# Attention on one core: the maxima turned later, the loads cut in four, two buffers of sums

## The chip, the cores and the metric

The kernel runs on one core of a Trainium2 chip. The metric is the device time of one execution, in microseconds. The core has TensorE (PE), VectorE (DVE), ScalarE (ACT), GpSimd (POOL), and SyncE (SP), which here issues nearly all transfers.

## The reference

One decoder layer on x of 2 x 2048 x 512 in fp32: causal self-attention, cross-attention over 77 rows, and a mixture of eight experts, each followed by a layer norm of x plus the result. Only the first is touched:

```python
qkv = x @ Wqkv.T
q, k, v = map(merge_heads, jnp.split(qkv, 3, axis=-1))     # 16 heads of 32
dots = jnp.einsum('bhid,bhjd->bhij', q, k) * dh ** (-0.5)
dots = jnp.where(causal_mask, -jnp.inf, dots)
out = jnp.einsum('bhij,bhjd->bhid', jax.nn.softmax(dots, axis=-1), v)
```

## The kernel before

Three stages follow one another: the projections to q, k and v, which go to DRAM in fp16 parts (`project`), the self-attention (`self_attention`), and everything after it (`chains`). The change is in the second.

The attention works on eight *groups*, each four heads of one batch. The group's q and k lie in one of two pairs of buffers (`q_pair`, `k_pair`), v in `v_sb`. Each of q and k is there in an upper and a lower fp16 part, so a product runs over 96 partitions. A group has four *chunks* of 512 queries; chunk c needs 4(c+1) tiles of 128 keys (`KU`), 40 tiles in all, and 160 *items*, one for each tile and head (`VU`).

Two streams run side by side on PE. The *value stream*, one item a step: PE computes scores with keys on partitions into `st_ps` (line 846), ACT takes the exponential into `probs` (line 743), PE multiplies by v into `o_ps` (line 866). The sums over keys: POOL adds two of three tiles of `probs` into `total` (line 630), PE takes the third tile, and `total` at the end of the chunk, with a column of ones into `den_ps` (lines 880 and 890). Five tiles of `probs` and three banks each of `st_ps` and `s_ps` are there.

The *aux stream* finds the row maxima some 70 items ahead: PE computes scores with queries on partitions into `s_ps` (line 829), DVE reduces them to `seg_max` (line 779). After the last maximum of a chunk comes the item `rows`: DVE takes the maximum over segments (line 783), scales it and splits it into two fp16 parts (lines 785 and 788), PE turns them by four fp16 products (line 818), DVE copies them to `max_rows` (line 775), and SP moves them into two more partitions of `q_pair` (line 671), so that the score product subtracts the maximum. `schedule()` spreads the aux items over the value steps by estimated costs; `done_by(s)` says how many are done by step s.

At the end of a chunk: ACT copies `o_ps` to `o_raw` and `den_ps` to `den`; SP moves `den` into a small layout (line 692), DVE takes reciprocals (line 797), SP stores them and loads them back broadcast as `inv` (lines 696 and 702), POOL multiplies (`o_sb`, line 640), ACT takes the upper fp16 part (line 758), POOL the lower one (line 645), SP stores both (line 709). The steps at which this happens, counted from the chunk's last item, are the constants `TAKEN` to `STORED`.

Order: every engine goes through the same steps in program order (`laps`), a lap of two groups, four times, and waits on semaphores. `chunk_at(s, lag)` tells whether step s lies `lag` steps after the last item of a chunk. Six steps after a group's end SP loads the group after the next into the buffers come free, 24 loads of 128 KB and one of 1 MB (lines 683 to 688).

Of the kernel before, what the change touches and what calls it, by code (L numbers as in the profile page):

```python
# [13 lines left out]
P = 128  # L14
KT = D // P
HG = P // DH
# [385 lines left out]
def self_attention(nc, S, x_rows, q_parts, k_parts, v_rows, o_parts, inv_rows):  # L402
# [16 lines left out]
    AUX = []  # L419
    for c in range(CPB):  # L420
        AUX += [("max", c, (j, h, s)) for j in range(TT) for h in range(HG) for s in range(c + 1)] + [("rows", c, None)]
# [17 lines left out]
    STORED = SCALED + 4  # L439
    TAIL = STORED + 1  # L440
    READY = 6
# [4 lines left out]
    def schedule():  # L446


        off = lambda c, kt: max(kt - c * TT, 0) * P
        steps = [0.06 + 0.6 * (CH - off(c, kt)) / CH for c, kt, _ in VU]  # L450
        busy = [0.0] * NVU
        for t in LAST_TILE:
            busy[(t * HG + HG - 1 + INVERTED) % NVU] += 0.2
        cost = []
        for what, c, unit in AUX:
            if what == "rows":
                cost.append(2.4)
# [78 lines left out]
    with ExitStack() as stack:  # L536
        sb = lambda *a: stack.enter_context(nc.sbuf_tensor(*a))
        ps = lambda *a: stack.enter_context(nc.psum_tensor(*a))
        q_pair = [sb(f"q_pair{a}", [NM, HG, T], F16) for a in range(2)]
# [3 lines left out]
        total = sb("total", [P, HG, CH], F32)  # L543
# [3 lines left out]
        ident16 = sb("ident16", [P, P], F16)  # L547
        future_f = sb("future_f", [P, 2, P], F32)
        future = sb("future", [P, 2, P], BF16)
        seg_max = sb("seg_max", [P, HG, TT, CPB], F32)  # L550
        row_max = sb("row_max", [P, HG, TT], F32)
        max_parts = sb("max_parts", [P, 2, HG, TT], F16)
        max_rows = sb("max_rows", [2 * HG, 2, CH], F16)
# [28 lines left out]
        steps = Count(nc, stack, "steps", 2 * 2 * CPB)  # L582
# [7 lines left out]
        def _(pool):  # L590
# [13 lines left out]
            nc.gpsimd.tensor_copy(ident16[:], ident_f[:]).then_inc(const_ready, 1)  # L604
            nc.gpsimd.tensor_copy(future[:], future_f[:]).then_inc(const_ready, 1)

            pool.wait_ge(const_ready, 3)
# [8 lines left out]
            def step(i, s, first, end):  # L616
                k = tile_at(s, 1, first, end)
                if k is not None and k % NKU in ADDS:
                    c, n = KU[k % NKU][0], adds_upto(k) - 1
                    starts = k % NKU == POOLED[c][1]  # L620
                    pool.wait_ge(exp_done.sem, exp_done.at(i, HG * k + HG - 1))
                    off = max(KU[k % NKU][1] - c * TT, 0) * P
                    if starts:

                        pool.wait_ge(den_ready.sem, den_ready.at(i, k // NKU * CPB + c - 1))
                        other = probs[:, (k // NKU * NKU + POOLED[c][0]) % NP]
                    else:
                        pool.wait_ge(added.sem, added.at(i, n - 1))
                        other = total[:]
                    last = nc.gpsimd.tensor_tensor(total[:, :, off:], other[:, :, off:], probs[:, k % NP, :, off:],  # L630
                                                   ALU.add)
                    if starts and off:
                        last = nc.gpsimd.tensor_copy(total[:, :, 0:off], other[:, :, 0:off])
                    last.then_inc(added.sem, 1)
                c = chunk_at(s, SCALED, first, end)
                if c is not None:

                    pool.wait_ge(inv_loaded, 16 * HG * (2 * CPB * i + c + 1))
# [3 lines left out]
                c = chunk_at(s, SCALED + 3, first, end)  # L642
# [8 lines left out]
        def _(sp):  # L651
            def load(g, a, c):
# [3 lines left out]
                for pair, parts, order in ((k_pair[a], k_parts, (0, 0, 1)), (q_pair[a], q_parts, (0, 1, 0))):  # L656
                    for r, part in enumerate(order):
                        sp.dma_start(pair[r * DH:(r + 1) * DH, :, c * CH:(c + 1) * CH],
                                     parts[part, bass.ds(f, P), cols].rearrange("(h p) n -> p h n", p=DH)).then_inc(
                                         qk_loaded[a][c], 16)  # L660
                if c == CPB - 1:
# [3 lines left out]
            def turn(i, n):  # L665
# [3 lines left out]
                at = c % CPB * CH  # L669
                for part in range(2):  # L670
                    sp.dma_start(q_pair[c // CPB % 2][NR + part:NR + part + 1, :, at:at + CH],
                                 max_rows[part * HG:(part + 1) * HG, c % 2]).then_inc(rows_moved[c % 2], 16)

            def step(i, s, first, end):
# [8 lines left out]
                k = tile_at(s, SUMS, first, end)  # L683

                if k is not None and k % NKU == NKU - 1 and end is None:
                    sp.wait_ge(pv_done.sem, pv_done.at(i, k))
                    for c in range(CPB):
                        load(2 * i + k // NKU + 2, k // NKU % 2, c)
# [10 lines left out]
                if c is not None:  # L699
                    sp.wait_ge(inv_stored, 16 * (2 * CPB * i + c + 1))  # L700
                    for h in range(HG):
                        sp.dma_start(inv[h * DH:(h + 1) * DH, c % 2], inv_rows[c % 2, h].partition_broadcast(
                            DH)).then_inc(inv_loaded, 16)
# [14 lines left out]
            for c in range(CPB):  # L718
                load(1, 1, c)
# [6 lines left out]
        def _(act):  # L726
# [3 lines left out]
            o_hi_done.lead(act)  # L730

            def step(i, s, first, end):
                p = unit_at(s, 0, first, end)
# [20 lines left out]
                c = chunk_at(s, SCALED + 2, first, end)  # L754
# [4 lines left out]

            laps(act, step)  # L760

        @block.vector
        def _(dve):
            for count in (s_read, max_ready, steps, recips):
                count.lead(dve)

            def aux(i, n):
# [4 lines left out]
                if what == "rows":  # L772

                    dve.wait_ge(rows_moved[k % 2], stored_at(2 * (CPB * i + k // 2)))
                    nc.vector.tensor_copy(max_rows[:, k % 2], s_ps[0:2 * HG, slot]).then_inc(s_read.sem, 1)
# [3 lines left out]
                nc.vector.reduce_max(seg_max[:, h, j, s:s + 1], s_ps[:, slot, 0:width], AX.X).then_inc(s_read.sem, 1)  # L779
                if AUX[(n + 1) % NAUX][0] == "rows":  # L780

                    dve.wait_ge(s_read.sem, s_read.at(i, n))
                    nc.vector.reduce_max(row_max[:], seg_max[:, :, :, 0:c + 1], AX.X).then_inc(steps.sem, 1)
                    dve.wait_ge(steps.sem, steps.at(i, 2 * k))
                    nc.vector.tensor_scalar(max_parts[:, 0], row_max[:], -1.0 / QK, None,
                                            ALU.mult).then_inc(steps.sem, 1)
                    dve.wait_ge(steps.sem, steps.at(i, 2 * k + 1))
                    nc.vector.scalar_tensor_tensor(max_parts[:, 1], row_max[:], -1.0 / QK, max_parts[:, 0], ALU.mult,
                                                   ALU.subtract).then_inc(max_ready.sem, 1)
# [14 lines left out]
        def _(pe):  # L804
# [3 lines left out]
            def aux(i, n):  # L808
# [18 lines left out]
                q0 = c * CH + j * P  # L827
                diagonal = s == c
                last = nc.tensor.matmul(s_ps[:, slot, 0:width], q_pair[a][0:NR, h, q0:q0 + P],  # L829
# [6 lines left out]
            def scores(i, p):  # L836
                c, kt, h = VU[p % NVU]
                a, slot = p // NVU % 2, p % (2 * NVU) % RING
                if kt == h == 0:
# [7 lines left out]
                                        q_pair[a][:, h, c * CH + off:(c + 1) * CH], start=True, stop=not diagonal)  # L847
# [35 lines left out]
            def totals(i, c):  # L883
# [5 lines left out]
                for h, out in enumerate(heads):  # L889
                    last = nc.tensor.matmul(den_ps[out, :], ones[:], total[:, h], start=opens, stop=True)  # L890
# [21 lines left out]
            pe.wait_ge(const_ready, 3)  # L912
# [672 lines left out]
```

## Time and profile before

| | us |
|---|---|
| median of three runs (2863.28 to 2868.97) | 2864.77 |
| the profiled execution | 2857.15 |
| its span | 2855.3 |
| PE busy in the span | 2498.4 |
| DVE, POOL, ACT busy | 1760.9, 1120.8, 1103.1 |

The page gives one profiled execution: the busy time of each engine, the span in slices, the chain that ended last, and the costliest groups of instructions. A timeline row is start, duration, engine, line, operation, operands, a count, and in brackets the engine's idle time before it with what ended it. A matmul's end is modelled.

### The profile page before, as it was taken

The numbers are of one execution on the slowest core, as the hardware profiler recorded it, in microseconds if no ns is written. First come the engines' busy times: TensorE is split into PE (matmuls) and PEld (weight loads), VectorE is DVE, ScalarE is ACT, GpSimd is POOL, SyncE is SP. The second block draws the span as 40 slices with busy tenths as digits, with TensorE's granted clock in tenths as the row PEclk, the third lists the DMA queues.
The fourth block names the chain that finished last, engine by engine and source line by source line (L and its number), as shares of the span: only waits on it lengthen the run. The fifth ranks groups of instructions, "written<-read, shape, count | busy, mean of one in ns | idle before, by whom it ended". The sixth has DMA issues, their size and how long they took to land. (4 is left out here: it accounts for less than half of the span.)

```text
span 2855.3 us, 43249 instructions
## 1 busy us (share of the span) xinstructions
PE 2498.4 (87%) x14164; PEld 1062.2 (37%) x14164; DVE 1760.9 (62%) x2997; ACT 1103.1 (39%) x2034; POOL 1120.8 (39%) x404
## 2 busy tenths in 40 slices
PE   8998787896969787887987569999999999999998
PEld 3443232232323232322331235444454445454543
DVE  5442865674747565665760538676767676777765
ACT  4231254553546454554555123233332323232420
POOL 0000386785858585876878212110201111111100
PEclk9999799897989898998998779999999999999999
DMA  7954403012030302022000310101010100101000
GB/s 239 312 182 140 108 17 68 24 25 64 14 75 17 73 17 67 20 48 73 9 24 8 137 41 1 42 16 42 16 42 16 42 16 7 51 1 56 1 15 15
DMA packets 130874, 155.58 MB, mean 54 GB/s; under 512 B 19966, under 2 KB 98558, under 8 KB 129629
## 3 DMA queue, kind: packets, MB, share of 16 engines
q1 hardware_dynamic: 130653, 152.69, 17.7%
q8 instruction: 132, 2.16, 0.3%
q14 instruction: 89, 0.73, 0.1%
HBM read 99.96 MB, written 52.17 MB: 53 GB/s over the span
## 5 line engine op out<-in xcount | busy, mean ns | idle before, releaser
L779 DVE TENSOR_REDUCE seg_max<-s_ps 128x1 f32<-128x512 f32 (+3 forms) x1280 | 707.1, 604 | 293.6 <-PE s_ps L829 202.9
L743 ACT ACTIVATE probs<-st_ps 128x512 f32<-128x512 f32 (+3 forms) x1280 | 611.0, 536 | 565.3 <-PE st_ps L846 353.6
L630 POOL TENSOR_TENSOR total<-total,probs 128x2048 f32<-128x2048 f32 (+3 forms) x200 | 705.7, 3528 | 98.1 <-ACT probs L743 86.2
L829 PE MATMUL s_ps<-k_pair,q_pair 96*128 96x512 f16 (+3 forms) x1280 | 450.9, 371 | 109.9 <-DVE seg_max L779 96.0
L846 PE MATMUL st_ps<-q_pair,k_pair 98*128 98x512 f16 (+3 forms) x1280 | 453.9, 370 | 70.3 <-ACT probs L743 61.7
L1410 PE MATMUL fps<-x2T,w_p_hi 128*128 128x512 f16 x1024 | 317.3, 379 | 0.0
L866 PE MATMUL o_ps<-probs,v_sb 128*32 128x512 f32 (+3 forms) x2560 | 316.3, 568 | 0.1
L1410 PE MATMUL fps<-w_p_hi,hT 128*128 128x512 f16 x1024 | 306.1, 381 | 0.0
L846 PEld LDWEIGHTS st_ps<-q_pair,k_pair 98*128 98x128 f16 x1280 | 125.1, 100 | 375.7 <-ACT probs L743 256.5
L1114 POOL TENSOR_TENSOR rstd<-rstd,keep_power 128x4 f32<-128x4 f32 x24 | 26.2, 1091 | 556.8 <-DVE rstd L1235 556.8
L829 PEld LDWEIGHTS s_ps<-k_pair,q_pair 96*128 96x128 f16 x1280 | 128.9, 102 | 300.5 <-DVE seg_max L779 223.1
L630 POOL TENSOR_TENSOR total<-probs 128x2048 f32<-128x2048 f32 (+1 forms) x32 | 136.2, 4255 | 230.0 <-PE den_ps L890 209.1
L1129 POOL TENSOR_TENSOR soft<-soft,ssum 128x1232 f32<-128x1232 f32 x32 | 72.9, 2289 | 385.9 <-DVE ssum L1265 385.9
L1372 DVE SCALAR_TENSOR_TENSOR x<-fps,gates_un,x 128x512 f32<-128x512 f32 x256 | 184.0, 746 | 36.0 <-PE fps L1410 33.0
L1197 ACT ACTIVATE hidden<-fps,keep_b_sb 128x512 f32<-128x512 f32 x128 | 86.5, 687 | 303.6 <-PE fps L1410 303.3
L1410 PE MATMUL fps<-w_p_lo,hT 128*128 128x512 f16 x512 | 194.6, 380 | 0.0
L1410 PE MATMUL fps<-x2T,w_p_lo 128*128 128x512 f16 x512 | 194.0, 379 | 0.0
L1361 DVE TENSOR_SCALAR hT<-hidden 128x512 f16<-128x512 f32 x128 | 86.1, 673 | 107.6 <-ACT hidden L1197 107.0
L1410 PEld LDWEIGHTS fps<-x2T,w_p_hi 128*128 128x128 f16 x1024 | 100.2, 98 | 128.8 <-issue 5.9
L1410 PEld LDWEIGHTS fps<-w_p_hi,hT 128*128 128x128 f16 x1024 | 98.1, 98 | 130.9 <-issue 20.7
L1168 ACT ACTIVATE soft<-soft 128x1232 f32<-128x1232 f32 x32 | 39.4, 1230 | 200.5 <-DVE soft L1258 200.5
L832 PE MATMUL s_ps<-future,ident_bf 128*128 128x128 bf16 x512 | 116.3, 228 | 0.0
(163 smaller groups left out, 3434.4 us busy)
## 6 DMA issues: line engine op xcount, KB each, us to landing
k_pair<-k_parts SPq DMA_DIRECT2D x96, 128.0 KB, 4.6
q_pair<-q_parts SPq DMA_DIRECT2D x96, 128.0 KB, 5.6
x_raw<-xT_in SPq DMA_DIRECT2D x8, 1024.0 KB, 6.2
q_parts<-qk_out SPq DMA_DIRECT2D x32, 256.0 KB, 3.6
k_parts<-qk_out SPq DMA_DIRECT2D x32, 256.0 KB, 4.0
piece_raw<-w_in SPq DMA_DIRECT2D x8, 1024.0 KB, 8.9
v_rows<-v_out SPq DMA_DIRECT2D x32, 256.0 KB, 2.1
w_parts<-piece_cut SPq DMA_DIRECT2D x8, 1024.0 KB, 5.8
```

The source lines that it names most:

```text
L630: last = nc.gpsimd.tensor_tensor(total[:, :, off:], other[:, :, off:], probs[:, k % NP, :, off:], ALU.add)
L743: nc.scalar.activation(probs[:, k % NP, h, off:], st_ps[:, p % (2 * NVU) % RING, off:], ACT.Exp, scale=SCALE).then_inc(exp_done.sem, 1)
L779: nc.vector.reduce_max(seg_max[:, h, j, s:s + 1], s_ps[:, slot, 0:width], AX.X).then_inc(s_read.sem, 1)
L829: last = nc.tensor.matmul(s_ps[:, slot, 0:width], q_pair[a][0:NR, h, q0:q0 + P], k_pair[a][0:NR, h, s * CH:s * CH + width], start=True, st ...
L832: last = nc.tensor.matmul(s_ps[:, slot, width - P:width], ident[:], future[:, 0], start=False, stop=True)
L846: last = nc.tensor.matmul(st_ps[:, slot, off:], k_pair[a][:, h, kt * P:(kt + 1) * P], q_pair[a][:, h, c * CH + off:(c + 1) * CH], start=Tr ...
L866: last = nc.tensor.matmul(o_ps[out, off:], v_sb[a][:, kt, out], probs[:, k % NP, h, off:], start=(kt == 0), stop=final)
L1129: nc.gpsimd.tensor_tensor(soft[:, j], soft[:, j], ssum[:, j, :].rearrange("p (h a) -> p h a", a=1).broadcast_to([P, H, S2]), ALU.mult).the ...
L1197: nc.scalar.activation(hidden[:, n % 2], fps[:, (u * NUNIT + f) % FB], ACT.Gelu, bias=W["b1_sb"][:, n:n + 1], scale=UN).then_inc(gelu_done ...
L1361: nc.vector.tensor_scalar(hT[:, 0, e % 2, j], hidden[:, n % 2], XS, None, ALU.mult).then_inc(h_hi.sem, 1)
L1372: nc.vector.scalar_tensor_tensor(x2[q][:, j], bank, gates_un[q][:, j, e:e + 1], x2[q][:, j], ALU.mult, ALU.add).then_inc(added.sem, 1)
L1410: last = nc.tensor.matmul(bank, lhs(a, t), rhs(b, t), start=(n == 0), stop=(n == len(steps) - 1))
```

## The change

- Loads of a group come in four parts, at `REFILLED`: 35, 55, 75 and 95 steps after the last item of the group whose buffers they fill; `v_sb` goes with the first part instead of the last. `q_pair` is laid out by chunk.
- `total` has two buffers, by the parity of the chunk; POOL waits for the sum of two chunks ago.
- The item `rows` of a chunk stands behind the first four maxima of the next chunk (`LATER`), but for the last chunk. `seg_max` has two buffers.
- The turn: PE transposes the fp32 maxima in one product (16 x 128). ACT writes the upper fp16 part to `max_rows` (`upper`), DVE the lower one in one operation. The old lines 785, 788 and 775 are gone. `max_rows` has 16 partitions of 128 columns, so the two row transfers have pieces of 256 B.
- `inv` is loaded by one transfer instead of four. The upper part of the output is taken 6 steps after `SCALED` instead of 2, the lower 8 instead of 3, and it is stored at 9 instead of 4. The planner's cost of a `rows` item is 1.0 (last chunk 2.0) instead of 2.4.

```diff
+    LATER = 4
     for c in range(CPB):
-        AUX += [("max", c, (j, h, s)) for j in range(TT) for h in range(HG) for s in range(c + 1)] + [("rows", c, None)]
+        items = [("max", c, (j, h, s)) for j in range(TT) for h in range(HG) for s in range(c + 1)]
+        AUX += items[:LATER] + [("rows", c - 1, None)] * (c > 0) + items[LATER:]
+    AUX.append(("rows", CPB - 1, None))
+    LAST_MAX = [max(n for n, x in enumerate(AUX) if x[:2] == ("max", c)) for c in range(CPB)]
...
-    STORED = SCALED + 4
+    UPPER = SCALED + 6
+    LOWER = UPPER + 2
+    STORED = LOWER + 1
     TAIL = STORED + 1
+    REFILLED = [TAIL + 20 * c for c in range(CPB)]
...
-                cost.append(2.4)
+                cost.append(1.0 if c < CPB - 1 else 2.0)
...
-                        pool.wait_ge(den_ready.sem, den_ready.at(i, k // NKU * CPB + c - 1))
+                        pool.wait_ge(den_ready.sem, den_ready.at(i, k // NKU * CPB + c - 2))
...
-                if c == CPB - 1:
+                if c == 0:
                     sp.dma_start(v_sb[a][:], v_rows[bass.ds(b * T, T), bass.ds(f, P)].rearrange(
...
-                    sp.dma_start(q_pair[c // CPB % 2][NR + part:NR + part + 1, :, at:at + CH],
-                                 max_rows[part * HG:(part + 1) * HG, c % 2]).then_inc(rows_moved[c % 2], 16)
+                    sp.dma_start(q_pair[c // CPB % 2][NR + part:NR + part + 1, c % CPB].rearrange("a h n -> a (h n)"),
+                                 max_rows[:, c % 2, part]).then_inc(rows_moved[c % 2], 16)
...
-                k = tile_at(s, SUMS, first, end)
-
-                if k is not None and k % NKU == NKU - 1 and end is None:
-                    sp.wait_ge(pv_done.sem, pv_done.at(i, k))
-                    for c in range(CPB):
+                for c in range(CPB):
+                    k = tile_at(s, REFILLED[c], first, end)
+                    if k is not None and k % NKU == NKU - 1 and (end is None or k < 0):
+                        sp.wait_ge(pv_done.sem, pv_done.at(i, k))
                         load(2 * i + k // NKU + 2, k // NKU % 2, c)
...
-                    for h in range(HG):
-                        sp.dma_start(inv[h * DH:(h + 1) * DH, c % 2], inv_rows[c % 2, h].partition_broadcast(
-                            DH)).then_inc(inv_loaded, 16)
+                    sp.dma_start(inv[:, c % 2], inv_rows[c % 2].rearrange("h (a n) -> h a n", a=1).broadcast_to(
+                        [HG, DH, CH])).then_inc(inv_loaded, 16)
...
+            def upper(i, n):
+
+                k = n // NAUX * CPB + AUX[n % NAUX][1]
+                slot = n % (2 * NAUX) % RING
+                act.wait_ge(s_ready.sem, s_ready.at(i, n))
+                act.wait_ge(rows_moved[k % 2], stored_at(2 * (CPB * i + k // 2)))
+                nc.scalar.activation(max_rows[:, k % 2, 0], s_ps[0:HG * TT, slot, 0:P], ACT.Copy,
+                                     scale=-1.0 / QK).then_inc(upper_ready.sem, 1)
+
             def step(i, s, first, end):
+                for n in aux_at(s, first, end):
+                    if AUX[n % NAUX][0] == "rows":
+                        upper(i, n)
                 p = unit_at(s, 0, first, end)
...
-                    dve.wait_ge(rows_moved[k % 2], stored_at(2 * (CPB * i + k // 2)))
-                    nc.vector.tensor_copy(max_rows[:, k % 2], s_ps[0:2 * HG, slot]).then_inc(s_read.sem, 1)
+                    dve.wait_ge(upper_ready.sem, upper_ready.at(i, k))
+                    nc.vector.scalar_tensor_tensor(max_rows[:, k % 2, 1], s_ps[0:HG * TT, slot, 0:P], -1.0 / QK,
+                                                   max_rows[:, k % 2, 0], ALU.mult,
+                                                   ALU.subtract).then_inc(s_read.sem, 1)
...
-                    for j in range(TT):
-                        last = nc.tensor.matmul(s_ps[0:2 * HG, slot, j * P:(j + 1) * P], max_parts[:, :, :, j],
-                                                ident16[:], start=(j == 0), stop=(j == TT - 1), skip_group_check=True)
-                    last.then_inc(s_ready.sem, 1)
+                    nc.tensor.transpose(s_ps[0:HG * TT, slot, 0:P], row_max[:].rearrange("p h j -> p (h j)"),
+                                        ident_f[:]).then_inc(s_ready.sem, 1)
```

## Rows read from the trace of the kernel before

**Rows 1.** The attention stage: length, busy of PE, PEld, DVE, ACT, POOL, clock, DMA

```profile
287.00:1583.00 1296.00, 1053.76 (x6976) 359.92 (x6976) 788.88 (x1440) 652.89 (x1376) 930.41 (x306) 0.90 0.17 41
```

**Rows 2.** Waits, 300 to 1570: total, times, longest

```profile
POOL total L630 <- PE den_ps L890: 209.1, 31, 20.5
...
DVE inv_small L797 <- DMA inv_small<-den: 112.1, 7, 17.2
...
ACT o_out L758 <- POOL o_sb L640: 75.3, 31, 4.8
...
PE s_ps L818 <- DVE max_parts L788: 29.9, 17, 3.0
...
PE den_ps L890 <- POOL total L630: 26.3, 9, 8.9
```

**Rows 3.** Timeline, SP and DVE, end of group 1

```profile
634.28 1.32 SPq L658 DMA_DIRECT2D k_pair<-k_parts  x3
...
648.44 6.24 SPq L692 DMA_DIRECT2D inv_small<-den  x1
...
658.63 0.25 DVE L797 RECIPROCAL inv_small<-inv_small 128x16 f32<-128x16 f32 x1 [17.19 <-DMA inv_small<-den]
```

**Rows 4.** First exponential to item 50: group 7, sum of groups 1 to 7

```profile
1426.10:1472.60 46.50, 38.59 (x264) 14.41 (x263) 26.79 (x50) 24.89 (x57) 35.95 (x16) 0.85 0.09 25
sum 425.40, PE 279.19 PEld 101.49 DVE 188.22 ACT 173.64 POOL 248.17; mean PE 39.88 PEld 14.50 DVE 26.89 ACT 24.81 POOL 35.45
```

**Rows 5.** DMA issues of the page; five microseconds of the load (last: GB/s)

```profile
650.00:655.00 5.00, 0.00 (x0) 0.00 (x0) 0.00 (x0) 0.00 (x0) 0.00 (x0) 0.50 1.05 219
...
v_sb<-v_rows SPq DMA_DIRECT2D x8, 1024.0 KB, 10.3
```

**Rows 6.** Timeline of ACT, POOL and SP, group 7, chunk 1; one window

```profile
1448.07 0.63 ACT L758 ACTIVATE o_out<-o_sb 128x512 f16<-128x512 f32 x1 [3.82 <-POOL o_sb L640]
...
1449.95 0.40 SPq L709 DMA_DIRECT2D o_parts<-o_out  x1
...
1451.41 4.51 POOL L630 TENSOR_TENSOR total<-total,probs 128x2048 f32<-128x2048 f32 x1 [1.48 <-ACT probs L743]
...
1457.91 8.10 POOL L630 TENSOR_TENSOR total<-total,probs 128x2048 f32<-128x2048 f32 x2 [2.00 <-ACT probs L743]
...
1465.97 1.26 POOL L640 TENSOR_TENSOR o_sb<-o_raw,inv 128x512 f32<-128x512 f32 x1
...
1467.27 0.63 ACT L758 ACTIVATE o_out<-o_sb 128x512 f16<-128x512 f32 x1 [4.61 <-POOL o_sb L640]
...
1468.66 0.49 ACT L743 ACTIVATE probs<-st_ps 128x128 f32<-128x128 f32 x2 [0.15 <-PE st_ps L849]
...
1450.00:1455.00 5.00, 5.00 (x19) 1.26 (x17) 2.43 (x5) 1.99 (x5) 3.59 (x1) 0.50 0.24 67
```

**Rows 7.** Timeline at a turn of maxima, group 1; two groups by shape

```profile
600.88 9.12 POOL L630 TENSOR_TENSOR total<-total,probs 128x2048 f32<-128x2048 f32 x2
...
606.62 3.41 DVE L785 TENSOR_SCALAR max_parts<-row_max 128x16 f16<-128x16 f32 x1
...
610.30 0.39 PE L818 MATMUL s_ps<-ident,max_parts 128*8 128x128 f16 x4 [2.96 <-DVE max_parts L788]
...
L788 DVE SCALAR_TENSOR_TENSOR max_parts<-row_max,max_parts 128x16 f16<-128x16 f32 x32 | 5.6, 176 | 1.1
...
L743 ACT ACTIVATE probs<-st_ps 128x128 f32<-128x128 f32 x128 | 29.8, 276 | 22.1 <-PE st_ps L849 21.1
```

**Rows 8.** PE's waits for POOL's sums in group 7; window of chunk 2

```profile
1517.21 1.94 PE L890 MATMUL den_ps<-total,ones 128*32 128x512 f32 x8 [3.69 <-POOL total L630]
...
1567.34 1.93 PE L890 MATMUL den_ps<-total,ones 128*32 128x512 f32 x8 [8.94 <-POOL total L630]
...
1477.70:1517.20 39.50, 33.73 (x223) 10.63 (x223) 23.38 (x39) 24.48 (x51) 36.57 (x11) 1.00 0.05 14
```

**Rows 9.** Timeline, PE's first score of the value stream

```profile
306.29 0.59 PE L846 MATMUL st_ps<-q_pair,k_pair 98*128 98x512 f16 x1 [5.59 <-issue]
```

More of the change, by code:

```diff
@@ L538, in self_attention @@
         ps = lambda *a: stack.enter_context(nc.psum_tensor(*a))
-        q_pair = [sb(f"q_pair{a}", [NM, HG, T], F16) for a in range(2)]
+        q_pair = [sb(f"q_pair{a}", [NM, CPB, HG, CH], F16) for a in range(2)]
         k_pair = [sb(f"k_pair{a}", [NM, HG, T], F16) for a in range(2)]
@@ L542, in self_attention @@
         probs = sb("probs", [P, NP, HG, CH], F32)
-        total = sb("total", [P, HG, CH], F32)
+        total = sb("total", [P, 2, HG, CH], F32)
         ones = sb("ones", [P, DH], F32)
@@ L546, in self_attention @@
         ident = sb("ident_bf", [P, P], BF16)
-        ident16 = sb("ident16", [P, P], F16)
         future_f = sb("future_f", [P, 2, P], F32)
         future = sb("future", [P, 2, P], BF16)
-        seg_max = sb("seg_max", [P, HG, TT, CPB], F32)
+        seg_max = sb("seg_max", [P, 2, HG, TT, CPB], F32)
         row_max = sb("row_max", [P, HG, TT], F32)
-        max_parts = sb("max_parts", [P, 2, HG, TT], F16)
-        max_rows = sb("max_rows", [2 * HG, 2, CH], F16)
+        max_rows = sb("max_rows", [HG * TT, 2, 2, P], F16)
         o_raw = sb("o_raw", [P, 2, CH], F32)
@@ L581, in self_attention @@
         max_ready = Count(nc, stack, "max_ready", 2 * CPB)
-        steps = Count(nc, stack, "steps", 2 * 2 * CPB)
+        upper_ready = Count(nc, stack, "upper_ready", 2 * CPB)
         recips = Count(nc, stack, "recips", 2 * CPB)
@@ L603, in _ @@
             nc.gpsimd.tensor_copy(ident[:], ident_f[:]).then_inc(const_ready, 1)
-            nc.gpsimd.tensor_copy(ident16[:], ident_f[:]).then_inc(const_ready, 1)
             nc.gpsimd.tensor_copy(future[:], future_f[:]).then_inc(const_ready, 1)
-            pool.wait_ge(const_ready, 3)
+            pool.wait_ge(const_ready, 2)
             nc.gpsimd.memset(k_pair[0][NR:NM], QK).then_inc(factors_ready, 1)
@@ L622, in step @@
                     off = max(KU[k % NKU][1] - c * TT, 0) * P
+                    summed = total[:, c % 2]
                     if starts:
-                        pool.wait_ge(den_ready.sem, den_ready.at(i, k // NKU * CPB + c - 1))
+                        pool.wait_ge(den_ready.sem, den_ready.at(i, k // NKU * CPB + c - 2))
                         other = probs[:, (k // NKU * NKU + POOLED[c][0]) % NP]
@@ L628, in step @@
                         pool.wait_ge(added.sem, added.at(i, n - 1))
-                        other = total[:]
-                    last = nc.gpsimd.tensor_tensor(total[:, :, off:], other[:, :, off:], probs[:, k % NP, :, off:],
+                        other = summed
+                    last = nc.gpsimd.tensor_tensor(summed[:, :, off:], other[:, :, off:], probs[:, k % NP, :, off:],
                                                    ALU.add)
                     if starts and off:
-                        last = nc.gpsimd.tensor_copy(total[:, :, 0:off], other[:, :, 0:off])
+                        last = nc.gpsimd.tensor_copy(summed[:, :, 0:off], other[:, :, 0:off])
                     last.then_inc(added.sem, 1)
@@ L636, in step @@
                 if c is not None:
-                    pool.wait_ge(inv_loaded, 16 * HG * (2 * CPB * i + c + 1))
+                    pool.wait_ge(inv_loaded, 16 * (2 * CPB * i + c + 1))
                     pool.wait_ge(split_done.sem, split_done.at(i, c - 1))
@@ L641, in step @@
                                             ALU.mult).then_inc(scaled.sem, 1)
-                c = chunk_at(s, SCALED + 3, first, end)
+                c = chunk_at(s, LOWER, first, end)
                 if c is not None:
@@ L655, in load @@
                 cols = bass.ds(b * T + c * CH, CH)
-                for pair, parts, order in ((k_pair[a], k_parts, (0, 0, 1)), (q_pair[a], q_parts, (0, 1, 0))):
+                for rows, parts, order in ((k_pair[a][:, :, c * CH:(c + 1) * CH], k_parts, (0, 0, 1)),
+                                           (q_pair[a][:, c], q_parts, (0, 1, 0))):
                     for r, part in enumerate(order):
-                        sp.dma_start(pair[r * DH:(r + 1) * DH, :, c * CH:(c + 1) * CH],
+                        sp.dma_start(rows[r * DH:(r + 1) * DH],
                                      parts[part, bass.ds(f, P), cols].rearrange("(h p) n -> p h n", p=DH)).then_inc(
                                          qk_loaded[a][c], 16)
-                if c == CPB - 1:
+                if c == 0:
                     sp.dma_start(v_sb[a][:], v_rows[bass.ds(b * T, T), bass.ds(f, P)].rearrange(
@@ L668, in turn @@
                 sp.wait_ge(s_read.sem, s_read.at(i, n))
-                at = c % CPB * CH
                 for part in range(2):
-                    sp.dma_start(q_pair[c // CPB % 2][NR + part:NR + part + 1, :, at:at + CH],
-                                 max_rows[part * HG:(part + 1) * HG, c % 2]).then_inc(rows_moved[c % 2], 16)
+                    sp.dma_start(q_pair[c // CPB % 2][NR + part:NR + part + 1, c % CPB].rearrange("a h n -> a (h n)"),
+                                 max_rows[:, c % 2, part]).then_inc(rows_moved[c % 2], 16)
             def step(i, s, first, end):
@@ L718, in _ @@
             for c in range(CPB):
-                load(1, 1, c)
+                if REFILLED[c] <= TAIL:
+                    load(1, 1, c)
             laps(sp, step)
@@ L730, in _ @@
             o_hi_done.lead(act)
+            upper_ready.lead(act)
+            def upper(i, n):
[5 more added lines that the diff above has]
+                                     scale=-1.0 / QK).then_inc(upper_ready.sem, 1)
             def step(i, s, first, end):
+                for n in aux_at(s, first, end):
+                    if AUX[n % NAUX][0] == "rows":
+                        upper(i, n)
                 p = unit_at(s, 0, first, end)
@@ L753, in step @@
                     nc.scalar.activation(den[:, c % 2], den_ps[:], ACT.Copy, scale=1.0 / XS).then_inc(den_taken.sem, 1)
-                c = chunk_at(s, SCALED + 2, first, end)
+                c = chunk_at(s, UPPER, first, end)
                 if c is not None:
@@ L758, in step @@
                     nc.scalar.activation(o_out[:, c % 2, 0], o_sb[:], ACT.Copy).then_inc(o_hi_done.sem, 1)
+            for n in range(AHEAD):
+                if AUX[n][0] == "rows":
+                    upper(0, n)
             laps(act, step)
@@ L763, in _ @@
         def _(dve):
-            for count in (s_read, max_ready, steps, recips):
+            for count in (s_read, max_ready, recips):
                 count.lead(dve)
@@ L778, in aux @@
                 width = CH if s < c else (j + 1) * P
-                nc.vector.reduce_max(seg_max[:, h, j, s:s + 1], s_ps[:, slot, 0:width], AX.X).then_inc(s_read.sem, 1)
-                if AUX[(n + 1) % NAUX][0] == "rows":
+                nc.vector.reduce_max(seg_max[:, k % 2, h, j, s:s + 1], s_ps[:, slot, 0:width], AX.X).then_inc(s_read.sem, 1)
+                if n % NAUX == LAST_MAX[c]:
                     dve.wait_ge(s_read.sem, s_read.at(i, n))
[L783 to L789, printed above, removed]
+                    nc.vector.reduce_max(row_max[:], seg_max[:, k % 2, :, :, 0:c + 1], AX.X).then_inc(max_ready.sem, 1)
             def step(i, s, first, end):
@@ L826, in aux @@
                 width = CH if s < c else (j + 1) * P
-                q0 = c * CH + j * P
                 diagonal = s == c
-                last = nc.tensor.matmul(s_ps[:, slot, 0:width], q_pair[a][0:NR, h, q0:q0 + P],
+                last = nc.tensor.matmul(s_ps[:, slot, 0:width], q_pair[a][0:NR, c, h, j * P:(j + 1) * P],
                                         k_pair[a][0:NR, h, s * CH:s * CH + width], start=True, stop=not diagonal)
@@ L846, in scores @@
                 last = nc.tensor.matmul(st_ps[:, slot, off:], k_pair[a][:, h, kt * P:(kt + 1) * P],
-                                        q_pair[a][:, h, c * CH + off:(c + 1) * CH], start=True, stop=not diagonal)
+                                        q_pair[a][:, c, h, off:], start=True, stop=not diagonal)
                 if diagonal:
@@ L889, in totals @@
                 for h, out in enumerate(heads):
-                    last = nc.tensor.matmul(den_ps[out, :], ones[:], total[:, h], start=opens, stop=True)
+                    last = nc.tensor.matmul(den_ps[out, :], ones[:], total[:, c % 2, h], start=opens, stop=True)
                 last.then_inc(den_ready.sem, 1)
@@ L910, in step @@
                     aux(i, n)
-            pe.wait_ge(const_ready, 3)
+            pe.wait_ge(const_ready, 2)
             for n in range(AHEAD):
```

## The prediction

> **What bounds the kernel now.** I read the page's slices first, then a row of busy time for the self-attention stage, then the waits of that stage, then the timeline around the largest ones. Only that stage is changed. It takes 1296 of 2855 us, and in it the busiest engine, TensorE (PE), is busy 1053.76 us; POOL 930.41, DVE 788.88, ACT 652.89 [rows 1]. So some 240 us of PE are idle, in few long gaps, and behind them POOL is the next engine: 930/8 = 116 us for each of the eight groups of heads, of about 162 us now (1296 / 8).
>
> The waits name the gaps [rows 2]. DVE waits 112.1 us in seven pieces for the denominators' small transfer; ACT waits 75.3 us for POOL's `o_sb`; PE waits 29.9 us for `max_parts` and 26.3 us for the added sums. POOL's 209.1 us for `den_ps` look largest, but most of them are the same 16 us stalls seen from POOL.
>
> In the rows below, *item n* is the n-th exponential (0 to 159) of a group; all five engines go through one program order of such steps.
>
> **1. Loads in four parts (lines 683 to 688 and 718).** Today, six items after a group ends, SP issues 25 transfers for the group after the next, from 634.28 on. The small transfer of the denominators stands behind them on SP and in the queues: issued at 648.44, it holds SP 6.24 us, and DVE has waited 17.19 us for it when it goes on at 658.63 [rows 3]. DVE is in program order, so no maxima are taken, PE has no free bank and stops. This happens in six groups (1 to 6; nothing is loaded in group 7; the seventh DVE wait, in group 7, is after its last maximum and holds up nobody). The price is in one view: the stretch from the first exponential of a group to item 50 holds the same work in groups 1 to 7 (264 PE instructions, 50 of DVE, 16 of POOL). The seven take 425.40 us together, group 7 alone, without a load, 46.50, so the six others 378.9, or 63.15 each [rows 4]. The difference, 6 x 16.65 = 100 us, holds the stall and the slow clock behind it: **-100**.
>
> The parts now start at items 34, 54, 74 and 94, when the first three small transfers of the previous chunk are through. The first part, for chunk 0, has 6 loads and the 1 MB of `v_sb`, 1.8 MB; at the burst's 219 GB/s [rows 5] that is 8 us, with 2 us of latency 10 (the `v_sb` load alone is 10.3 us from issue to landing at the median, with the burst ahead of it [rows 5]). Behind it on SP is `inv` of chunk 0, at item 36. What this costs is counted in 2. The second part (0.8 MB, 4 us) precedes by three items the denominators of chunk 1, which DVE wants six items, 5 us, later: 0 taken, 4 us x 6 groups as the other end. No maxima of the group loaded are due before item 90 for part one and item 104 for part two, so no part is late for PE.
>
> **2. UPPER four items later, LOWER five.** In each group ACT stops at items 27 and 42 for POOL (3.82 and 4.61 us in group 7 [rows 2, 6]), PE with it, and the granted clock falls to 1.2 GHz behind it (0.50 from 1450 to 1455 [rows 6]). Are four items of slack enough? I follow POOL in group 7. After item 23 it does one add, then `o_sb` of the previous chunk, done just before ACT's 1448.07: ACT, which would be at item 30 at about 1447.5, then loses 0.6 instead of 3.8. Then the next add (4.5), the split (1.2) and two adds (4.5, 3.5) run without the 1.5 and 2.0 us of idleness of today [rows 6], `o_sb` of chunk 0 ends at about 1464.5 instead of 1467.2 (1465.97 + 1.26), and ACT, at item 46 by 1459, waits 5 us all the same. Item 46 started at 1468.7 [rows 6], so a group gains 4 us, not 8: this stretch is POOL's. In groups 1 to 6 the load takes most of that back: SP reaches it only when POOL's split lets it store (LOWER, at 1455.2 in this count, against 1449.95 now), it needs 3.2 us to issue, and `inv` lands behind 10 us of loads, at about 1466.5, 3.3 us after POOL wants it (1464.5 less its own 1.3). Taken: groups 0 and 7 gain 4 each, the six others 0.7 each: **-12**. The ends: 0, and 8 x (4.6 + 3.3 us of half clock) = -63, if ACT no longer stops at all.
>
> **3. The turn of the maxima.** Four items later, the row maxima are there before PE asks, except in the last chunk, which has gaps in its plan. L785 goes: it holds DVE 3.41 us at 606.62 and ends exactly where POOL's second add does (600.88 + 9.12 = 610.00), and PE waits 2.96 [rows 7]. Such waits are 29.9 us in the stage [rows 2], and I take 27 of them, since the last chunk's turn keeps part of its wait. PE's transposition is one fp32 product instead of four fp16: no change taken. DVE loses the copy of line 775 and L788 and gets one operation of 128 columns from PSUM, nearest to L788's 0.18 us [rows 7]. DVE's new operation has one operand in SBUF and one in PSUM, as I read it with no wait for POOL. **-27**.
>
> The Trainium skill bears on this (SBUF — State Buffer, "SBUF: two separate sides"): DVE and GpSimd share one port pair under an exclusive lock held for a whole instruction, taken by DVE in its two-port modes or with two SBUF inputs. The 3.41 us agree. By the rule the new operation never waits for POOL; were it held by POOL like L785, most of the 27 us would stay lost, and the sum would be 2750.
>
> What is added: `upper`, an ACT copy of 16 x 128, 32 times, nearest to the 128 x 128 exponential of 0.276 us [rows 7], 9 us on ACT, which is idle half the stage. It stands before an exponential and waits for PE's item of the same step, and DVE waits for ACT. PE runs up to three units ahead, so mostly nothing; I take 0.25 us each: **+8**, between 0 and 32 x 2.96 = 95, the wait that this same turn costs today.
>
> **4. Two buffers of sums.** POOL need not wait for the previous chunk's sum. But its first add needs item 7, 23, 55 or 103, and `den_ps` is ready at that very item; so only about 1 us a chunk opens. PE waits for POOL's sum at item 103 (3.69 us in group 7) and 8.94 us at the very end [rows 8]. POOL's chunk 2 is 36.57 us of work in 39.50 [rows 8], so 1 us a group is won, and 2 at the end by an earlier last chunk; one `inv` transfer instead of four saves SP three issues there. **-10** (0 to -26).
>
> **5. The start.** The first score waits 5.59 us, till 306.29 [rows 9], for the row transfer of chunk 0, which stands behind the loads. As many bytes are ahead of it after the change, `v_sb` only earlier among them: **+1**, 0 to +5.
>
> **Rows in 256 B pieces.** The two row transfers now have 16 pieces each instead of four of 1 KB. The DMA: Bandwidth & Descriptors page of the Trainium skill, "Specifications", puts the least size for full rate at 512 B, with read-modify-write below. No row shows the size alone. Only the last chunk has so little slack (issue at item 90, use at 96) that it would tell. If each of the eight took 2 us longer, it would be 16 us, inside my range.
>
> **Sum.** -100 - 12 - 27 - 10 + 8 + 1 = -140. The profiled execution took 2857.15 us (span 2855.3 and 1.85 around it): 2717. The median of three, 2864.77, is 7.6 above it, so 2725.
>
> **The rivals.**
> *A. ACT no longer stops.* If POOL is faster to `o_sb` than I count, -63 instead of -12: 2674. For it: POOL idles 3.5 us in that stretch today. Against: 20.8 us of POOL work between items 23 and 46 (4.5 + 1.3 + 4.5 + 1.2 + 4.5 + 3.5 + 1.3), for 22 items of some 0.76 us ((46.5 - 3.8 - 4.6) / 50 [rows 4, 6]). Chance 0.10.
> *B. The parts still stall.* Each first part makes POOL, and each second part DVE, 4 us later than I count: 6 x 8 = 48, so 2773. For it: the queues are seen to be in order, and the small transfers stand close behind. Chance 0.17.
> *C, the other side. The turn becomes a ring.* PE waits for DVE's maxima, ACT for PE, DVE for ACT, and the next exponentials are behind ACT's wait. At 2.96 us for each of 32 turns it is 87 more, 2812. From (140 + 8)/32 = 4.6 us each, the kernel is slower than before; at 5.5 us it is 2893. For it: ACT's waits for POOL are of that length. Against: PE's lead, and the earlier row maxima. Chance 0.06, half of it beyond 4.6 us.
> *D. Nothing changes*, since POOL bounds the whole stage: then 8 x 116 = 930 us would have to be near 1296, which it isn't. 0.01.
>
> **The numbers.** My forecast has 0.66, with 2690 to 2760 as its own range. 2675 to 2805 takes in most of A and B and the ends of 2 to 4. A measurement can't tell less than 0.2%, 6 us, from no change: faster 0.66 + 0.10 + 0.17 + 0.03 = 0.96, same 0.01, slower 0.03.
>
> **What would show it.** 1: no DVE wait for `inv_small` over 3 us before the last chunk, and the six stretches to item 50 at 46 to 50 us. 2: ACT's wait for `o_sb` once a group, about 5 us or more, at item 46; POOL waiting for `inv` in groups 1 to 6. 3: no wait of PE for `row_max`, `upper` near 0.3 us, DVE's new operation near 0.2 with no 3 us among them. 4: PE's wait at item 103 still 1 to 3 us. I am wrong if the stretches to item 50 stay above 55 us, or if a new wait of PE, ACT or DVE around `s_ps` comes 32 times.

## The result and the profile after

| | before, us | after, us |
|---|---|---|
| median of four runs each | 2864.03 | 2722.05 (2719.72 to 2723.16) |
| the profiled execution, its span | 2857.15, 2855.3 | 2722.91, 2721.1 |
| granted clock, mean | 0.934 | 0.947 |

The ratio is 0.9507, 95% interval 0.9482 to 0.9532: 5% faster. The forecast was 2725.

The self-attention stage as one window [rows 1], then the stretches from the first exponential to item 50 of groups 1, 6 and 7 and the sum of groups 1 to 7 [rows 4]. The columns are those of before.

```profile
286.80:1452.80 1166.00, 1023.74 (x6881) 352.08 (x6882) 727.72 (x1376) 653.86 (x1408) 928.45 (x307) 0.93 0.18 46
```

```profile
456.80:502.00 45.20, 34.39 (x259) 13.07 (x257) 26.03 (x48) 24.09 (x57) 32.99 (x14) 0.92 0.22 60
...
1156.40:1207.60 51.20, 34.26 (x260) 13.02 (x257) 26.02 (x48) 24.24 (x57) 32.92 (x14) 0.88 0.32 94
1301.10:1339.60 38.50, 34.21 (x260) 13.02 (x259) 25.93 (x48) 24.23 (x57) 33.02 (x14) 0.98 0.07 23
sum 317.40, PE 244.16 PEld 92.22 DVE 182.54 ACT 169.91 POOL 231.17; mean PE 34.88 PEld 13.17 DVE 26.08 ACT 24.27 POOL 33.02
```

The stage is 130 us shorter, nearly all of the 134 of the span. The seven stretches went from 425.4 to 317.4. Without group 7 (46.5, now 38.5) the six with loads lost 378.9 - 278.9 = 100.0 us.

The waits of the stage, 300 to 1440 [rows 2]:

```profile
ACT o_out L775 <- POOL o_sb L645: 79.2, 16, 17.6
DVE inv_small L813 <- DMA inv_small<-den: 66.0, 3, 48.3
POOL o_sb L645 <- DMA inv<-inv_rows: 45.2, 8, 12.3
PE den_ps L903 <- POOL total L635: 31.1, 9, 10.6
DVE max_rows L795 <- ACT max_rows L743: 19.1, 21, 1.4
```

DVE's seven waits for `inv_small` are three: 48.3 of the 66 us are at the end of the stage and 16.6 in the last chunk of group 7, where no load is due. PE's wait for `max_parts` has no successor. What is new is POOL's wait for `inv` in groups 1 to 6 (the wait of 11.31 us at the stage's end, at 1446, lies outside this window). ACT stops 16 times instead of 31 and for about as long in all (79.2 us, 75.3 before [rows 2]): the stops of groups 1 to 7 at item 46, of 5.1 to 17.6 us, hold nearly all of it. One such stop, from the timelines of SP, POOL, ACT and PE at item 46 of group 1:

```profile
484.99 0.41 SPq L712 DMA_DIRECT2D o_parts<-o_out  x1
485.88 1.34 SPq L664 DMA_DIRECT2D k_pair<-k_parts  x3
487.31 1.74 SPq L664 DMA_DIRECT2D q_pair<-q_parts  x3
489.29 0.40 SPq L668 DMA_DIRECT2D v_sb<-v_rows  x1
489.83 2.65 SPq L705 DMA_DIRECT2D inv<-inv_rows  x1
498.99 1.26 POOL L645 TENSOR_TENSOR o_sb<-o_raw,inv 128x512 f32<-128x512 f32 x1 [6.26 <-DMA inv<-inv_rows]
500.38 0.63 ACT L775 ACTIVATE o_out<-o_sb 128x512 f16<-128x512 f32 x1 [11.47 <-POOL o_sb L645]
501.23 0.61 PE L859 MATMUL st_ps<-q_pair,k_pair 98*128 98x512 f16 x1 [10.60 <-ACT probs L760]
```

The small transfer stands behind the 1 MB of `v_sb`, and POOL goes on 9.2 us after its issue. POOL stands idle 6.26 us, ACT 11.47, PE with it 10.60. In group 6 two loads of the next stage (`keep_x`, `keep_oT`) are issued ahead of `inv` as well, and POOL waits 12.27 us, ACT 17.65.

The turn, by line [rows 7]:

```profile
L795 DVE SCALAR_TENSOR_TENSOR max_rows<-s_ps,max_rows 16x128 f16<-16x128 f32 x32 | 8.9, 279 | 20.8 <-ACT max_rows L743 19.1 <-PE s_ps L845 1.3 <-PE s_ps L842 0.3
L743 ACT ACTIVATE max_rows<-s_ps 16x128 f16<-16x128 f32 x32 | 8.3, 260 | 34.7 <-PE s_ps L833 33.0
```

### The profile page after: what moved, and what is told of

Same layout as the page of the kernel before. It is cut to its first block and busy times, and to the rows that moved or that the text cites. A ratio compares the mean times of both kernels' runs of the same rounds, so it can differ in the third digit from the quotient of the medians.

```text
span 2721.1 us, 42945 instructions
## 1 busy us (share of the span) xinstructions
PE 2465.9 (91%) x14068; PEld 1054.1 (39%) x14068; DVE 1700.1 (62%) x2933; ACT 1103.9 (41%) x2066; POOL 1119.1 (41%) x403
## 5 line engine op out<-in xcount | busy, mean ns | idle before, releaser
L879 PE MATMUL o_ps<-probs,v_sb 128*32 128x512 f32 (+3 forms) x2560 | 310.0, 558 | 0.1
```

The lines of the kernel that those rows point to most:

```text
L879: last = nc.tensor.matmul(o_ps[out, off:], v_sb[a][:, kt, out], probs[:, k % NP, h, off:], start=(kt == 0), stop=final)
```

## Experiments

Each is timed against the kernel before on the same chip; in brackets the ratio to it with its 95% interval. Differences from "after" are from its 2722.05; since the kernel before took 2864.0 to 2867.9 beside the various runs, they are good to some 4 us.

**e1_first_late.** The first part of the loads goes behind `inv`.

```diff
-    REFILLED = [TAIL + 20 * c for c in range(CPB)]
+    REFILLED = [TAIL + 20 * c + 6 * (c == 0) for c in range(CPB)]
```

> After, with the first part of the loads six items later (item 40 instead of 34), so that SP issues chunk 0's inv before it. Theory (the stop of ACT at item 46, 11.5 us in group 1, is inv behind v_sb): the stop falls to the 4 us of group 7, so stretches to item 50 fall from 45.2 to 38.5 us in groups 1 to 5, 5 x 6.7 = 34 us less; in group 6 two loads of the next stage stay ahead of inv. 2722 - 34 = 2688. Rival (it is POOL's own adds that hold ACT there): stretches stay at 45 us, 2722.

Measured: 2677.55 (0.9341, 0.9313 to 0.937), 44 below after and 10 more than the theory gave. POOL's wait for `inv` (the 11.4 here is the one at the stage's end, which the 45.2 of after does not hold, so 11.1 are left of 45.2, 8.84 of them in group 6):

```profile
POOL o_sb L645 <- DMA inv<-inv_rows: 22.5, 5, 11.4
```

The first part in front of `inv` cost the changed kernel 44 us. From one first exponential to the next, groups 1 to 5 together took 699.6 us and take 662.0, 7.5 less each, group 6 2.9 less. In the five, ACT's stop at item 46 is 5.1 to 6.8 us shorter; the rest fits the slow clock behind such a stop (0.50 from 502 to 507 in after), but was not measured apart.

**e2_parts_only.** The kernel before, with only its loads cut in four parts.

```diff
+    REFILLED = [TAIL + 20 * c for c in range(CPB)]
...
+                for c in range(CPB):
+                    k = tile_at(s, REFILLED[c], first, end)
```

> Before, with the loads in four parts (at items 29, 49, 69, 89) and nothing else of the change. Theory (the burst was one stall of 16.65 us in each of six groups): -100, and +3 us a group for inv of chunk 0 behind the first part: 2864 - 82 = 2782, DVE's waits for inv_small gone. Rival (the parts shift the stall to ACT, which stops at item 42 as long as inv is late, 8 us a group): 2864 - 52 = 2812.

Measured: 2770.76 (0.9657, 0.9623 to 0.9691), -94 where the theory gave -82 and the rival -52. The parts alone, `v_sb` with the first of them, are two thirds of the gain. The old turn's rows of this kernel (line, count, busy, mean ns) come back under e4:

```profile
L786 DVE TENSOR_SCALAR max_parts<-row_max 128x16 f16<-128x16 f32 x32 | 44.8, 1400 | 1.8 <-DVE row_max L784 0.8
...
L789 DVE SCALAR_TENSOR_TENSOR max_parts<-row_max,max_parts 128x16 f16<-128x16 f32 x32 | 5.6, 175 | 1.1
```

**e3_upper_early.** The later UPPER undone.

```diff
-    UPPER = SCALED + 6
-    LOWER = UPPER + 2
-    STORED = LOWER + 1
+    UPPER = SCALED + 2
+    LOWER = UPPER + 1
+    STORED = LOWER + 6
```

> After, with the upper and lower parts of the output taken at 2 and 3 steps behind SCALED as before (stored at 9 as after). Theory (the slack is worth 8 us a group where inv is in time and covers the stop at item 27 only where it is late): +8 in groups 0 and 7 and +4 to 6 in the six others, 2722 + 45 = 2767. Rival (the stops are POOL's in any order, as counted in the prediction, 4 us a group): 2722 + 12 = 2734.

Measured: 2738.24 (0.9554, 0.9523 to 0.9585), +16: near the rival's number, but not 4 us in each group. From its first exponential to its last, group 7 takes 130.2 us instead of 122.3. From one first exponential to the next, groups 1, 3 and 5 take 140.1, 140.0 and 139.9 as in after, groups 4 and 6 1 us more, group 0 2.7 more, and group 2 147.0 instead of 140.0. So the four items are worth 8 us in group 7, where nothing is loaded, and next to nothing in five of the six groups with a load; why group 2 is the exception wasn't looked into.

**e4_old_turn.** After, with the old operations of the turn (scaling and split on DVE from SBUF, four fp16 products, the copy), still four items later.

```diff
+                    nc.vector.tensor_scalar(max_parts[:, 0], row_max[:], -1.0 / QK, None, ...
+                    nc.vector.scalar_tensor_tensor(max_parts[:, 1], row_max[:], -1.0 / QK, max_parts[:, 0], ...
-                    nc.tensor.transpose(s_ps[0:HG * TT, slot, 0:P], row_max[:].rearrange("p h j -> p (h j)"), ...
```

> After, with the old operations of the turn (scale and split on DVE in lines 785 and 788, four fp16 products, copy of 8 x 512), still four items later than the last maximum. Theory (the delay alone takes PE's wait away, DVE's 3.4 us are then beside other work): 0 to +8 us, 2722 to 2730, L785 still up to 3.4 us long. Rival (it is the held DVE that costs, wherever PE's item stands): the 27 us come back, 2749.

Measured: 2808.94 (0.9818, 0.9778 to 0.9859), +87: more than either theory gave. Its groups by line, then POOL, DVE and PE at one turn:

```profile
L795 DVE SCALAR_TENSOR_TENSOR max_parts<-row_max,max_parts 128x16 f16<-128x16 f32 x32 | 40.3, 1261 | 1.1
L792 DVE TENSOR_SCALAR max_parts<-row_max 128x16 f16<-128x16 f32 x32 | 39.7, 1241 | 1.1
```

```profile
542.95 8.00 POOL L638 TENSOR_TENSOR total<-total,probs 128x2048 f32<-128x2048 f32 x2
543.06 4.42 DVE L795 SCALAR_TENSOR_TENSOR max_parts<-row_max,max_parts 128x16 f16<-128x16 f32 x1
547.53 0.59 PE L825 MATMUL s_ps<-ident,max_parts 128*8 128x128 f16 x4 [4.55 <-DVE max_parts L795]
```

The operation with two SBUF inputs, 176 ns before [rows 7], is held for 4.42 us, until POOL's first add ends (547.48). It is held so in 17 of 32 turns, each time to the end of a POOL instruction; in before, where it stood right behind the held L785, it never was (at most 177 ns). This is the lock of the Trainium skill (SBUF — State Buffer, "SBUF: two separate sides"); the trace agrees. While DVE is held, the maxima stand still: PE waits 43.0 us for `seg_max` (5.7 in after) and 24.9 for `max_parts` (none in after).

**e5_one_total.** One buffer of sums.

```diff
-                        pool.wait_ge(den_ready.sem, den_ready.at(i, k // NKU * CPB + c - 2))
+                        pool.wait_ge(den_ready.sem, den_ready.at(i, k // NKU * CPB + c - 1))
```

> After, with one buffer of added sums and POOL's wait for the previous chunk's sum as before. Theory (the first add needs the exponentials of the item at which den_ps is ready, so the second buffer opens about 1 us a chunk, and little of it reaches PE): +2 to +10 us, 2724 to 2732. Rival (POOL is close to the bound now, and the wait feeds into ACT's stop and PE's wait at item 103 in every chunk): 3 us a group more, 2746.

Measured: 2724.77 (0.9502, 0.9482 to 0.9521), +2.7, less than can be told from nothing; the spans are 2721.4 and 2721.1. The second buffer is worth 0 to 3 us.

**e6_inv_four.** `inv` by four transfers of 32 partitions, as before.

```diff
+                    for h in range(HG):
+                        sp.dma_start(inv[h * DH:(h + 1) * DH, c % 2], inv_rows[c % 2, h].partition_broadcast(DH)) ...
```

> After, with inv loaded by four transfers of 32 partitions again. At the end of the stage the single transfer takes 5.07 us from issue to POOL's start, the four before took 3.32. Theory (one transfer of 128 repeated rows is itself slow): 1.7 us less at the end and 1.7 us in each of six groups where POOL waits for inv: 2722 - 12 = 2710. Rival (what it waits for is the queue ahead, and the four issues cost SP 1.3 us): 2722, with 3.3 us at the end alone.

Measured: 2711.21 (0.9452, 0.9433 to 0.9471), -11. The last `inv` of the stage, of after and of e6:

```profile
1440.93 0.53 SPq L705 DMA_DIRECT2D inv<-inv_rows  x1
...
1446.00 1.26 POOL L645 TENSOR_TENSOR o_sb<-o_raw,inv 128x512 f32<-128x512 f32 x1 [11.31 <-DMA inv<-inv_rows]
```

```profile
1432.24 1.71 SPq L706 DMA_DIRECT2D inv<-inv_rows  x4
1435.57 1.26 POOL L645 TENSOR_TENSOR o_sb<-o_raw,inv 128x512 f32<-128x512 f32 x1 [9.61 <-DMA inv<-inv_rows]
```

From issue to POOL it is 5.07 us with one transfer, 3.33 with four. In groups 1 to 6 POOL's wait is 0.8 to 1.3 us shorter with four. The single transfer costs.

**e7_turn_at_once.** The new turn, not delayed: `LATER = 0`.

> After, with the item rows directly behind the last maximum of its chunk, as before, and the new operations of the turn. The old operations four items later gave 2809. Theory (what DVE executes decides, since it is held by POOL, and not where PE's item stands): 0 to +8 us, 2722 to 2730. Rival (both are needed, PE waits for row_max, then DVE for ACT, about 1 us for each of 32): 2754.

Measured: 2737.56 (0.9545, 0.9525 to 0.9564), +15.5, between the two. DVE's wait for ACT's upper part is 52.9 us, longest 5.9, instead of 19.1, longest 1.4. The delay is worth about a tenth of the change.

**e8_upper_later.** `UPPER = SCALED + 12`, and with it the loads six items later; the landing of `inv` is counted by two semaphores, one for each buffer.

> After, with UPPER 12 items after SCALED instead of 6; all parts of the loads, and the first loads of the next stage, move six items with it, behind inv of chunk 0; inv has two semaphores for it. Theory (with inv in time ACT's stop at item 46 is POOL's lag of some 5 us, which six more items cover, and group 6 loses its 10 us of loads in front of inv): 2678 of the run with the first part late, less 8 x 4 and 8: 2638. Rival (POOL bounds chunk 1, ACT then stops for probs and PE for the sums instead): 2665 to 2678.

Measured: 2668.3 (0.9303, 0.9284 to 0.9322). The rival's number, from another cause. ACT's stops for `o_sb` are gone, but PE has a new wait. The waits, then DVE, POOL, SP and PE in group 2:

```profile
PE st_ps L859 <- DMA q_pair<-max_rows: 41.1, 8, 7.4
...
PE den_ps L903 <- POOL total L635: 20.2, 6, 10.6
```

```profile
654.43 0.28 DVE L795 SCALAR_TENSOR_TENSOR max_rows<-s_ps,max_rows 16x128 f16<-16x128 f32 x1 [1.36 <-ACT max_rows L743]
...
659.06 1.15 POOL L650 TENSOR_TENSOR o_out<-o_sb,o_out 128x512 f16<-128x512 f32 x1
...
660.42 0.42 SPq L712 DMA_DIRECT2D o_parts<-o_out  x1
660.99 1.21 SPq L676 DMA_DIRECT2D q_pair<-max_rows  x2
...
663.54 0.61 PE L859 MATMUL st_ps<-q_pair,k_pair 98*128 98x512 f16 x1 [5.94 <-DMA q_pair<-max_rows]
```

SP waits in order for POOL's split (till 660.2) before it stores `o_parts`. The maxima behind it, written by DVE at 654.71, are moved 6.3 us after that.

**e9_stored_later.** e8 with the store three items later (`STORED = LOWER + 4`).

> The run with UPPER 12 items after SCALED, with SP's store of the output three steps later, so that SP issues the row transfers of the last chunk (step 89) before it waits for POOL's split of chunk 1 (store at 90 instead of 87). Theory (the 3.7 to 7.4 us that PE waits at item 96 for the rows are SP standing in that wait): 8 x 5 us and some slow clock go, 2668 - 40 = 2628, PE's wait for the rows gone. Rival (the 256 B pieces or the chain over ACT and DVE make the rows late): 2668.

Measured: 2668.59 (0.9317, 0.9287 to 0.9347), not 40 us less. The wait for the rows is gone (0.9 us), and this has grown from 20.2:

```profile
PE den_ps L903 <- POOL total L635: 51.1, 14, 10.6
```

In groups 2 and 4 PE is also idle 7.3 to 7.7 us at item 44 for no cause that the profile names.

**e10_spread.** e9, `inv` by four transfers, and the load cut in five, each behind a small transfer, `v_sb` alone.

```diff
-    REFILLED = [TAIL + 20 * c for c in range(CPB)]
+    REFILLED = [TAIL, TAIL + 6, TAIL + 49, TAIL + 79, TAIL + 32]
```

> As the run with the store three steps later, and inv in four transfers, and the parts placed by what follows them on SP: chunk 0 at item 43, chunk 1 at 49, v at 75, chunk 2 at 92, chunk 3 at 122. Theory (a part costs only where a small transfer stands right behind it): 2 us at the end, 1 to 2 a group, 2628 - 12 = 2616. Rival (the parts are hidden already): 2626. This is the candidate for the fastest version.

Measured, five rounds: 2634.21 (2631.81 to 2638.78; 0.92, 0.9175 to 0.9224). It is the fastest, 3.2% below after, and 34 us below e9, more than the 12 that the theory gave; its edits were not run one by one. PE's largest wait in it, the pace of ACT and DVE apart, is for POOL's sums:

```profile
PE den_ps L905 <- POOL total L635: 40.4, 14, 10.6
```

**e11_turn_only.** The kernel before, with only the new turn, its delay and its planner costs.

> Before with only the turn of the maxima changed: new operations, four items later, the planner's new costs; one burst of loads, one buffer of sums, UPPER and LOWER at 2 and 3, inv in four. Theory of the prediction (the turn is worth PE's 29.9 us of waits less 8): 2864 - 19 = 2845, with the burst stalls of 16 us there. Rival (the turn is worth what the old operations cost in the run that had all else, 87 us, because DVE was the next limit everywhere): 2777 to 2800.

Measured: 2833.27 (0.9893, 0.9861 to 0.9925), -33: 12 below the theory and far from the rival.

**e12_old_turn_at_once.** The change without its turn: old operations, `LATER = 0`, cost 2.4.

> After, with all of the old turn: its operations, directly behind the last maximum, and the planner's old cost of 2.4. So it is the change without its turn. Theory (how long POOL holds DVE's two small operations hangs on where they fall among POOL's adds; the delay made it worse with the old operations): parts alone gave 2771, UPPER is worth 16 in after, so 2755, and the second operation, held 40 us in all in the run four items later, near 6 us again. Rival (the old operations cost some 80 us wherever they stand once the other stalls are gone): 2800.

Measured: 2839.66 (0.9901, 0.9873 to 0.9929), +118, beyond the rival too. Groups by line, and PE's wait:

```profile
L792 DVE TENSOR_SCALAR max_parts<-row_max 128x16 f16<-128x16 f32 x32 | 76.3, 2385 | 1.1
L795 DVE SCALAR_TENSOR_TENSOR max_parts<-row_max,max_parts 128x16 f16<-128x16 f32 x32 | 49.6, 1550 | 1.1
...
L825 PE MATMUL s_ps<-ident,max_parts 128*8 128x128 f16 x128 | 16.0, 265 | 102.5 <-DVE max_parts L795 102.5
```

So the turn is worth 33 us alone and 118 on top of the rest. Shown is that the old operations now meet POOL's instructions far more often: 52 of the 64 are held over 0.4 us, each to the end of a POOL instruction, and they take 125.9 us of DVE, against 20 of 64 and 50.4 us in e2. Open is why: e12 is e2 with the later UPPER, the later store and loads, two sums, the single `inv` and the new layout of `q_pair`, and is 69 us slower. Which of these brings the adds onto the turn wasn't run.

## Why the forecast was right, and where it was not

- **Step 1 (-100): right.** e2 gives -94. No DVE wait for `inv_small` is over 3 us before the last chunk.
- **Steps 1 and 2 in the six groups:** -17.35 each was forecast, 100.0 / 6 = -16.7 came, out of two mis-sized terms. The stretches were to be 46 to 50 us and are 45.2 to 45.8, and 51.2 in group 6. (a) "a group gains 4 us, not 8": group 7 gained 8.0 and lost 8 again in e3. ACT did wait, 5.07 us at item 46, as the "5 us all the same" had it. But POOL's `o_sb` ended 36.9 us after the group's first exponential instead of 41.1, 4.3 us earlier where 2.7 were counted, and ACT, already through items 43 to 46 when it stopped, was at item 50 soon after. (b) "`inv` lands ... 3.3 us after POOL wants it": 6.1 to 6.8 in groups 1 to 5, and ACT, which waits on POOL, stops 7.5 to 12.0 us there; e1 gives 7.5 us for each of the five. Both ends were in the prediction (-63, rival B), but as unlikely ones, when each was in part true.
- **Step 3 (-27 + 8): right in kind, too small.** DVE's new operation takes 279 ns in all 32 (at most 280), though 23 of them lie wholly inside a POOL instruction; it was to be near 200. PE never waits for the row maxima, ACT's copy takes 260 ns as forecast. Of the coupling of 8 us, PE shows little: ACT waited 2.4 us in the stage, PE 2.3 us for `max_rows`. DVE waited 19.1 us for ACT's upper part, 21 times, which comes near the prediction's own sign of being wrong (a new wait 32 times) but holds up nobody for long. The term was priced by PE's waits in before. Alone the turn gives -33, not -19, and on top of the rest -118: PE's waits for the old parts are 32.8 us in the whole run of before and 102.5 in e12. What the old turn costs depends on the other stalls, and the sum took it as fixed.
- **Step 4 (-10): wrong.** "one `inv` transfer instead of four saves SP three issues": it does, and POOL goes on 1.7 us later at the end of the stage and 0.8 to 1.3 us later in six groups, +11 (e6). The second buffer gives 0 to 3. PE's wait at item 103 was still 2.0 to 2.7 us in groups 1 to 6 and 4.0 in group 7, its sum 31.1 us instead of 26.3 [rows 2].
- **Step 5 (+1):** the first score came 3.3 us earlier, at 302.98; why wasn't looked into.
- **Rows in 256 B pieces:** no effect is seen. The row transfers land in 1.7 / 1.8 / 5.2 us (least, median, most; the trace of before gives no landing of its rows), and PE waits 0.6 us for them in the stage, as in before. The full-rate size of the Trainium skill (DMA: Bandwidth & Descriptors, "Specifications") has no cost that these 4 KB transfers show.
- **Rivals:** A is refuted for after (2722, not 2674; ACT stops in all of groups 1 to 7), though group 7 gained A's 8 us with ACT still stopping for 5; e8, where ACT no longer stops, is near its number (2668), with PE's new wait for the rows in it. B is half true: POOL comes late in groups 1 to 6, while DVE waits 1.1 us in all of them. C is refuted.

The sum, -140 forecast for -134 in the span, is right in its largest term. The rest is luck: the stop behind the first part (44 us) and the single `inv` (11) were priced too low, group 7's gain and the turn too low on the other side, and these misses cancel. The terms don't add up either: the change without its turn (e12) is only 28 us below before, and the turn alone 33, yet together they are 142.

## What to carry to other kernels

Ask of every small transfer what bulk load stands before it on its queue, and of every waiting store what stands behind it on the issuing engine; here moving one load by six items gave 44 us. A tiny DVE operation with its inputs in SBUF cost, beside a busy GpSimd, up to a whole GpSimd instruction (4.42 us here), and how often can't be read from a kernel with other stalls (20 of 64 in before, 52 in e12): the new one, with one input in PSUM, stayed at 279 ns. A removed stop hands its time to the next late resource (ACT's stop to the row transfer to POOL's sums), so price what is late next before adding up the gain.

## What the hardware did that was not expected

- One broadcast transfer of 128 rows of 2 KB took 5.07 us to POOL, four of 32 rows 3.33.
- Tiny DVE operations (128 x 16) with their inputs in SBUF averaged 1.2 to 2.4 us in e4 and e12, against 0.18 us for L788 in before.
- PE has a gap for which the profile names no cause, in groups 2 and 4, at the item where `laps` starts its loop's body again: 2.63 and 2.33 us at item 35 in after, 2.2 to 3.9 over the other runs in which it can be told, and 7.3 to 7.7 in e9, where the first part of the loads is issued just before. In before none stands out. That the branch is the cause, and in e9 the load, is only argued.
